# Decoder layer, expert stage: gate and up products with the expert's weights as stationary operand

## The chip, the cores and the metric

One NeuronCore of one Trainium2 chip runs the whole program in one launch. The metric is the device time of one execution in microseconds (us), the median of three runs. A product here is one matmul on TensorE: a stationary operand of 128x128 is loaded into the array (LDWEIGHTS), then the moving operand streams through, column by column, and the sum goes to a bank of PSUM.

## The reference, cut to what matters

One post-norm decoder layer on 32 sequences of 64 tokens (2048 tokens, width 512): self attention, cross attention, then a mixture of experts. Only the last part is touched.

```python
scores = jax.nn.sigmoid(x @ gate_w.T) + bias
topk_w, topk_idx = jax.lax.top_k(scores, TOPK)          # 4 of 16 experts
topk_w = topk_w / (jnp.sum(topk_w, axis=-1, keepdims=True) + 1e-20)
cw = jnp.sum(jax.nn.one_hot(topk_idx, E, dtype=x.dtype) * topk_w[..., None], axis=1)
g = jnp.einsum('th,eih->eti', x, Wg)                    # h 512, i 256
u = jnp.einsum('th,eih->eti', x, Wu)
z = jax.nn.silu(g) * u
zw = z * cw.T[:, :, None]
out = jnp.einsum('eti,ehi->th', zw, Wd)
out = out + jax.nn.silu(x @ Sg.T) * (x @ Su.T) @ Sd.T
```

## The kernel before, in words

Every product is made of three float16 ones: each operand is split into a high and a low half, and `three_pass` (lines 284 to 291) adds high by high (line 288), high by low (289) and low by high (290) into one bank, for each block of the contraction.

The expert stage works on 79 tiles of 128 picks, sorted by expert; each tile belongs to one expert. Which expert that is, is known only on the chip, since the routing has just computed it. The weights of four experts lie in a ring in SBUF (`m.ring`; per expert `2 * EW` elements, high half then low half). Table `m.place` says at which offset of the ring the tile's expert stands. TensorE's sequencer reads an entry of it into a register (`weights`, line 2041: a table load and two more operations), and every slice of the weights is addressed by that register plus a constant, which costs the sequencer an address operation in its instruction stream (ISA in the listings below, FUSED_REGOPS in the trace).

All 79 steps are written out, one after the other. Step s on TensorE, in this order:
- `gate_and_up(s)` (line 2043 on): waits for the tile's turned tokens `m.xth`, `m.xtl` (lines 2050, 2051), then 12 products with the tokens as stationary operand (128 features x 128 tokens) and 512 columns of weights moving (256 of gate, 256 of up), into one bank `GU`. After the first six the place of the next tile is loaded.
- `turn_rows` for tile s + 2 (line 1509): eight products with an identity turn the gathered rows of tokens, into `XH` and `XL`. They wait for the gather and for the copies of the last turning (lines 2088, 2089).
- `down(s - 1)` (line 2060 on): waits for zh and zl of the tile before, then six products, weights moving, 512 columns, into bank `Y`.
- `turn_z(s)` (line 2070 on): waits for z, then two float32 products with an identity turn z, tokens by features, into features by tokens, in bank `ZT`.

Beside it, in this order per step, ScalarE: silu of the gate half out of `GU` (line 1991), copy of `XH` to `m.xth` (1997), every other step Y times the pick's weight (2000), copy of `ZT` to zh (2002). VectorE: z = up times silu (2015), copy of `XL` to `m.xtl` (2019), the pick's weight (2022, 2024), every other step Y (2028), zl = `ZT` - zh (2030). GpSimd issues the gather of rows for tile s + 4 (1499) and the scatter-add of Y (1977). SyncE loads the next expert's weights (1495) when a ring slot is free, that is when TensorE has ended the last tile of the expert that had it; table `m.free` holds the event count for that.

The order between engines is kept by one counting semaphore per engine (`Timeline`): each engine marks its events in a fixed order, and others wait for a count.

Of the kernel before, what the change touches and what calls it, by code (L numbers as in the profile page):

```python
# [24 lines left out]
P = 128  # L25
# [4 lines left out]
KD = D // P  # L30
# [4 lines left out]
NE, TOPK, FI = 16, 4, 256  # L35
IB = FI // P
# [60 lines left out]
def events(per_step, extra=(), steps=NQ):  # L97

    out = []
    for q in range(steps):  # L100
        for name in per_step:
            out.append((q, name))
            for qq, after, names in extra:
                if qq == q and after == name:
                    out += [(q, x) for x in names]
    return out


def build(nc, x, xT, cT, maskf, wqT, wkT, wvT, b3, woT, bo, xwq, xwk, xwv, xwo,
# [3 lines left out]
    with top:  # L113
# [3 lines left out]
        def sem(name):  # L117
            return top.enter_context(nc.semaphore(name))
# [1397 lines left out]
        def route_and_shared(m, ln, ctx):  # L1516
# [135 lines left out]
            def vector(dve):  # L1652
# [128 lines left out]
                wait(dve, PE, "owners")  # L1781
                then(dve.tensor_copy(own[:, :], bank[1][0:1, 0:NTILES + 2]))
                dve.tensor_scalar(m.need[:, :], own[:, :], 16.0, 16.0, ALU.mult, ALU.add)
                dve.tensor_scalar(m.free[:, :], end[0:1, :], 4.0, 19.0, ALU.mult, ALU.add)
                floor_of_quotient(third[:, :], own[:, :], RING)
                then(dve.scalar_tensor_tensor(own[:, :], third[:, :], -float(RING), own[:, :], ALU.mult, ALU.add))
                dve.memset(m.place[:, 0:1], 0)
# [105 lines left out]
        def experts(m, ln):  # L1893
# [3 lines left out]
            with ExitStack() as ctx:  # L1897
# [4 lines left out]
                zh, zl = ([b(f"{n}{j}", [P, IB, P], F16) for j in range(2)] for n in ("zh", "zl"))  # L1902
                yo = [raw_front[:, j * D:(j + 1) * D] for j in range(U)]
                s_yo = [sem(f"mo_s_yo{j}") for j in range(U)]
                XH, XL, GU, ZT, Y = bank[0], bank[1], [bank[2], bank[3]], [bank[4], bank[5]], [bank[6], bank[7]]

                def per_step(names, odd):

                    return [(q, n) for q in range(U) for n in names if n != "y" or q % 2 == odd]
                PE = Timeline(sem("mo_pe"), events(["gu", "turn", "y", "zt"], steps=U), 0, [], U)  # L1910
                AC = Timeline(sem("mo_act"), per_step(["si", "xh", "y", "zh"], 1), 0, [], U)
                DV = Timeline(sem("mo_dve"), per_step(["z", "xl", "wp", "ws", "y", "zl"], 0), 0, [], U)
                assert LAST.q % 2
# [5 lines left out]
                def turns(s):  # L1919

                    return s + 2 < NTILES
# [19 lines left out]
                @block.sync  # L1941
                def _(sp):
                    routing.sync(sp)
                    routing.wait(sp, routing.DV, "tables")
                    for e in range(RING, NE):
                        sp.wait_ge(m.s_w, 16 * e)
                        done = sp.value_load(m.free[0:1, e - RING:e - RING + 1], min_val=23, max_val=4 * NTILES + 19)
                        sp.wait_ge(PE.sem, done)
                        met(sp)
                        expert_weights(sp, m, e)  # L1950
                    sp.wait_ge(m.s_w, 16 * NE)
                    combined.sync(sp, s_yo)
# [29 lines left out]
                @block.scalar  # L1982
                def _(act):
                    routing.scalar(act)
                    AC.start(act)
                    routing.wait(act, routing.DV, "tables")

                    for s in range(NTILES):
                        st, par = step(s), s % 2
                        act.wait_ge(PE.sem, PE.value("gu", st))  # L1990
                        AC.mark(act.activation(sg[par][:, :], GU[par][:, 0:FI], ACT.Silu, scale=1 / WS), "si", st, () if turns(s) else ("xh",))  # L1991
                        if turns(s):
                            loaded = act.value_load(m.need[0:1, s + 2:s + 3], min_val=16, max_val=16 * NE)
                            act.wait_ge(m.s_w, loaded)
                            met(act)
                            act.wait_ge(PE.sem, PE.value("turn", st))
                            AC.mark(act.activation(m.xth[par][:, :, :].rearrange("p k t -> p (k t)"), XH[:, :], ACT.Copy), "xh", st)
                        if out_of(st) is AC:
                            act.wait_ge(PE.sem, PE.value("y", st))
                            AC.mark(act.activation(stored(act, s - 1)[:, :], Y[(s + 1) % 2][:, :], ACT.Copy, scale=weight(act, s - 1)), "y", st)  # L2000
                        act.wait_ge(PE.sem, PE.value("zt", st))
                        AC.mark(act.activation(zh[par][:, :, :].rearrange("p n t -> p (n t)"), ZT[par][:, 0:FI], ACT.Copy), "zh", st)
                    act.wait_ge(PE.sem, PE.value("y", LAST))
                    AC.mark(act.activation(stored(act, NTILES - 1)[:, :], Y[(NTILES + 1) % 2][:, :], ACT.Copy, scale=weight(act, NTILES - 1)),
                            "si", LAST, ("xh", "y"))
                    combined.scalar(act)

                @block.vector
                def _(dve):
                    routing.vector(dve)  # L2010
                    DV.start(dve)
                    for s in range(NTILES):
                        st, par = step(s), s % 2
                        dve.wait_ge(AC.sem, AC.value("si", st))
                        i = dve.scalar_tensor_tensor(z[par][:, :], GU[par][:, FI:2 * FI], OS / WS, sg[par][:, :], ALU.mult, ALU.mult)  # L2015
                        DV.mark(i, "z", st, () if turns(s) else ("xl", "wp", "ws"))
                        if turns(s):
                            dve.wait_ge(PE.sem, PE.value("turn", st))
                            i = dve.tensor_copy(m.xtl[par][:, :, :].rearrange("p k t -> p (k t)"), XL[:, :])
                            DV.mark(i, "xl", st)  # L2020
                            t = s + 2
                            DV.mark(dve.tensor_tensor(m.of_pick[:, t % 2, :], weights_of(m, t), m.which[:, t, :], ALU.mult), "wp", st)
                            dve.wait_ge(DV.sem, DV.value("wp", st))
                            i = dve.tensor_reduce(m.weight[:, t % U:t % U + 1], m.of_pick[:, t % 2, :], AX.X, ALU.add)
                            DV.mark(i, "ws", st, ("y",) if s == 0 else ())
                        if out_of(st) is DV and s:
                            dve.wait_ge(PE.sem, PE.value("y", st))
                            DV.mark(dve.tensor_scalar(stored(dve, s - 1)[:, :], Y[(s + 1) % 2][:, :], weight(dve, s - 1), None, ALU.mult), "y", st)
                        dve.wait_ge(AC.sem, AC.value("zh", st))
                        DV.mark(dve.tensor_tensor(zl[par][:, :, :].rearrange("p n t -> p (n t)"), ZT[par][:, 0:FI],  # L2030
                                                  zh[par][:, :, :].rearrange("p n t -> p (n t)"), ALU.subtract), "zl", st)
                    combined.vector(dve)

                @block.tensor
                def _(pe):
# [7 lines left out]
                    def gate_and_up(s, w):  # L2043

                        st, par = step(s), s % 2
                        if s < 2:
                            routing.wait(pe, routing.AC, f"xh{s}")
                            routing.wait(pe, routing.DV, f"xl{s}")
                        else:
                            pe.wait_ge(AC.sem, AC.value("xh", st, 2))  # L2050
                            pe.wait_ge(DV.sem, DV.value("xl", st, 2))
                        n = 2 * FI
                        pairs = [(m.xth[par][:, k, :], m.xtl[par][:, k, :], w[:, k * n:(k + 1) * n], w[:, EW + k * n:EW + (k + 1) * n])
                                 for k in range(KD)]
                        three_pass(pe, GU[par][:, :], pairs[:2], stop=False)
                        following = weights(s + 1) if s + 1 < NTILES else None
                        mm = three_pass(pe, GU[par][:, :], pairs[2:], start=False)
                        PE.mark(mm, "gu", st, () if turns(s) else ("turn",))
                        return following

                    def down(s, w, before=()):
# [4 lines left out]
                                                            w[:, EW + c + n * D:EW + c + (n + 1) * D]) for n in range(IB)])  # L2066
                        names = (*before, "y")
                        PE.mark(mm, names[0], st, names[1:])

                    def turn_z(s):  # L2070
                        st, par = step(s), s % 2
                        pe.wait_ge(DV.sem, DV.value("z", st))
                        for n in range(IB):
                            mm = pe.transpose(ZT[par][:, n * P:(n + 1) * P], z[par][:, n * P:(n + 1) * P], ident[:, :])  # L2074
                        PE.mark(mm, "zt", st)

                    routing.wait(pe, routing.DV, "tables")
                    pe.wait_ge(m.s_w, 32)
# [1 line left out]
                    for s in range(NTILES):  # L2080
# [11 lines left out]
                        if s:  # L2092
# [2 lines left out]
                            tl = out_of(st)  # L2095
                            pe.wait_ge(tl.sem, tl.value("y", st, 2))
                            down(s - 1, before)
                        turn_z(s)
                        before, w = w, following
                    tl = out_of(LAST)  # L2100
                    pe.wait_ge(tl.sem, tl.value("y", LAST, 2))
                    down(NTILES - 1, before, ("gu", "turn"))

        def combine_and_normalise(m):

# [215 lines left out]
```

## Time and profile before

| what | value |
|---|---|
| median of three runs | 1801.9 us (1801.45 to 1802.96) |
| span of the profiled execution, first to last instruction | 1799.8 us |
| what lies around the span, by the median | 2.1 us |
| mean granted TensorE clock | 0.980 of full speed |
| TensorE busy | 1704.9 us, 95% of the span |
| expert stage, first to last product on expert weights | 1391.4 to about 1758.5 us |

The span is that of one execution; the profiled execution has no total of its own beside it, so the 2.1 us are the difference to the median of the three timed runs. A product's duration in the trace includes its way through the array: one with 512 columns shows 0.38 us, but the next starts 0.216 us after it. So the pace is read from the distance between starts. Of a sequencer's instructions, which the busy columns don't count, the duration is what it executes, and again the distance between starts is what it costs.

### The profile page before, as it was taken

Reading aid. Unit: us, or ns where it says so; the run is one execution under the profiler, and the core shown is the slowest. Engines: PE = TensorE matmul, PEld = TensorE weight load, DVE = VectorE, ACT = ScalarE, POOL = GpSimd, SP = SyncE. Lnnn points to the kernel's source line nnn. Section 1 sums busy time; section 2 is a strip of 40 time slices with the busy share of each in tenths; the row PEclk is TensorE's granted clock in tenths of the full one; section 3 lists DMA queues with packets and bytes.
Section 4 is the critical chain, followed back from the end, with each engine's and each line's share of the span. In section 5 each row is a group of like instructions: output and inputs, shape, how many; then the busy total and the mean of one; then the engine's idle time right before and its main releaser. Section 6 shows DMA issues by size and latency. Waiting matters only on the chain. (4 is left out here: it accounts for less than half of the span.)

```text
span 1799.8 us, 38774 instructions
## 1 busy us (share of the span) xinstructions
PE 1704.9 (95%) x15285; PEld 983.5 (55%) x15285; DVE 1318.8 (73%) x2251; ACT 919.3 (51%) x1545; POOL 899.9 (50%) x731
## 2 busy tenths in 40 slices
PE   6999999899999999999999999999799999899990
PEld 4676766465555555555555555555454555455550
DVE  5778789678888888888888888888879444444445
ACT  5566656665646564555455555555731333333335
POOL 7643034555645555546455555465531555555550
PEclk9999999999999999999999999999989999999995
DMA  9720020211412213214122131122144678887669
GB/s 253 173 49 20 8 62 3 92 68 53 131 61 98 85 63 98 85 58 131 64 79 87 43 104 62 56 87 70 66 165 138 152 153 217 204 225 153 118 101 298
DMA packets 84945, 190.40 MB, mean 106 GB/s; under 512 B 10848, under 2 KB 29664, under 8 KB 82720
## 3 DMA queue, kind: packets, MB, share of 16 engines
q1 hardware_dynamic: 61104, 129.44, 21.3%
q0 software_dynamic: 23088, 58.37, 16.0%
q8 instruction: 126, 2.06, 0.5%
q14 instruction: 51, 0.42, 0.1%
q10 hardware_dynamic: 576, 0.11, 0.0%
HBM read 124.68 MB, written 63.21 MB: 104 GB/s over the span
## 5 line engine op out<-in xcount | busy, mean ns | idle before, releaser
L288 PE MATMUL bank<-xhl,front_h 128*128 128x512 f16 x704 | 269.4, 383 | 11.6 <-DVE front_l L409 10.5
L289 PE MATMUL bank<-xhl,front_h 128*128 128x512 f16 x704 | 269.0, 382 | 0.0
L290 PE MATMUL bank<-xhl,front_l 128*128 128x512 f16 x704 | 268.8, 382 | 0.0
L1047 POOL TENSOR_TENSOR xa_xs<-xa_xs,sn 128x512 f32<-128x512 f32 x160 | 232.0, 1450 | 45.8 <-ACT xa_xs L1099 45.8
L1058 POOL TENSOR_TENSOR xa_sc<-xa_sc,xa_rs 128x1024 f32<-128x1024 f32 x32 | 60.8, 1901 | 374.1 <-DVE xa_rs L1312 374.1
L1052 POOL TENSOR_TENSOR xa_rr<-xa_x,xa_xs 128x512 f32<-128x512 f32 x160 | 233.1, 1457 | 12.7 <-DVE xa_x L1207 0.2
L288 PE MATMUL bank<-out_h,xa_oh 128*128 128x512 f16 x512 | 194.1, 379 | 10.7 <-DVE xa_ol L1189 7.0
L1977 POOL DMA_INDIRECT scratch_y<-raw_front,moe_to x79 | 125.3, 1586 | 144.9 <-DVE mo_zl L2030 119.7
L290 PE MATMUL bank<-out_h,xa_ol 128*128 128x512 f16 x512 | 194.0, 379 | 0.0
L289 PE MATMUL bank<-out_l,xa_oh 128*128 128x512 f16 x512 | 194.0, 379 | 0.0
L1098 ACT ACTIVATE xa_xs<-bank 64x512 f32<-64x512 f32 x160 | 94.9, 593 | 131.0 <-PE bank L290 126.7
L1207 DVE TENSOR_TENSOR xa_x<-bank,cs 128x512 f32<-128x512 f32 x160 | 109.5, 686 | 64.8 <-ACT xa_xs L1099 60.2
L1212 DVE TENSOR_TENSOR xa_rql<-xa_rr,xa_rqh 128x512 f16<-128x512 f32 x128 | 141.5, 1105 | 12.2 <-ACT xa_rqh L1105 11.6
L1155 ACT ACTIVATE xa_sc<-xa_sc 128x512 f32<-128x512 f32 x64 | 40.2, 629 | 205.9 <-DVE xa_sc L1227 205.9
L2015 DVE SCALAR_TENSOR_TENSOR raw_out<-bank,raw_out 128x256 f32<-128x256 f32 x79 | 33.6, 425 | 149.9 <-ACT raw_out L1991 143.5
L288 PE MATMUL bank<-moe_ring,moe_xth 128*128 x316 | 119.8, 379 | 0.0
L289 PE MATMUL bank<-moe_ring,moe_xth 128*128 x316 | 119.8, 379 | 0.0
L290 PE MATMUL bank<-moe_ring,moe_xtl 128*128 x316 | 119.8, 379 | 0.0
L288 PEld LDWEIGHTS bank<-xhl,front_h 128*128 128x128 f16 x704 | 69.3, 98 | 90.5 <-issue 14.0
L290 PEld LDWEIGHTS bank<-xhl,front_l 128*128 128x128 f16 x704 | 69.3, 99 | 84.7 <-issue 2.8
L1199 DVE SCALAR_TENSOR_TENSOR acc<-bank,acc 128x512 f32<-128x512 f32 x128 | 85.8, 671 | 37.1 <-PE bank L290 37.1
L289 PEld LDWEIGHTS bank<-xhl,front_h 128*128 128x128 f16 x704 | 69.4, 99 | 78.4 <-issue 2.2
(304 smaller groups left out, 4670.1 us busy)
## 6 DMA issues: line engine op xcount, KB each, us to landing
xa_rawc<-in_ew SPq DMA_DIRECT2D x32, 768.0 KB, 5.6
moe_ring<-scratch_w SPq DMA_DIRECT2D x16, 1536.0 KB
scratch_w<-xa_chunk_h SPq DMA_DIRECT2D x32, 384.0 KB, 2.3
scratch_w<-xa_chunk_l SPq DMA_DIRECT2D x32, 384.0 KB, 3.3
raw_front<-in_xwq SPq DMA_DIRECT2D x8, 1024.0 KB, 7.9
raw_out<-in_xwo SPq DMA_DIRECT2D x8, 1024.0 KB, 5.3
scratch_y<-xa_zero SPq DMA_DIRECT2D x18, 256.0 KB, 5.8
acc<-in_x POOLq DMA_DIRECT2D x4, 1024.0 KB, 10.0
```

The costliest lines, as they stand in the source:

```text
L288: pe.matmul(out_ap, ah, bh, start=start and m == 0, stop=False)
L289: pe.matmul(out_ap, ah, bl, start=False, stop=False)
L290: mm = pe.matmul(out_ap, al, bh, start=False, stop=stop and m == n - 1)
L1047: PO.mark(pool.tensor_tensor(xr, xr, sn[:, :].rearrange("p (a s) -> p a s", a=1) .to_broadcast([P, QT // S, S]), ALU.mult), f"sm{r}", st)
L1052: PO.mark(pool.tensor_tensor(rr[r % 2][:, :], x0[r % 3][:, :], xs[r % 3][:, :], ALU.add), f"ra{r}", st)
L1058: PO.mark(pool.tensor_tensor(s4, s4, rs[:, :, :].rearrange("p h (t a) -> p (h t) a", a=1) .to_broadcast([P, 16, S]), ALU.mult), "nm", st)
L1098: act.activation(xs[r % 3][0:64, :], src[64:128, :], ACT.Copy)
L1155: AC.mark(act.activation(s2, s2, ACT.Exp, scale=float(HD2) ** -0.5), f"ex{h}", st, ("ch",) if (i, q, h) == (NG - 1, NQ - 1, 1) else ())
L1199: DV.mark(dve.scalar_tensor_tensor(row, home[f"w{t}"][:, :], 1 / (WS * OS), row, ALU.mult, ALU.add), f"w{t}", st, also)
L1207: DV.mark(dve.tensor_tensor(xr, home_of(r, st)[:, :].rearrange("p (a s) -> p a s", s=S), cs[:, :].rearrange("p (a s) -> p a s", a=1) .to_b ...
L1212: DV.mark(dve.tensor_tensor(rotated(rkl, rql, r), rr[r % 2][:, :].rearrange("p (a s) -> p a s", s=S), rotated(rkh, rqh, r), ALU.subtract), ...
L1977: pool.indirect_dma_start((ya, yb)[t % 2][:, :], bass.IndirectOffsetOnAxis(m.to[:, t:t + 1], 0), y[:, :], None, compute_op=ALU.add).then_i ...
```

## The change

Gate and up swap their operands. The weights are now stationary (128 features of the input x 128 features of the output), the tile's turned tokens move (128 columns). So g and u come out as features by tokens, which is how the down products want z, and nothing turns z any more: `turn_z` and the bank pair `ZT` go. Gate gets a bank of its own and an event of its own ("g"), up another. ScalarE makes zh from z itself, VectorE subtracts it from z. The order of events on TensorE is now g, gu, turn, y, so the count in `m.free` moves by one.

```diff
-                XH, XL, GU, ZT, Y = bank[0], bank[1], [bank[2], bank[3]], [bank[4], bank[5]], [bank[6], bank[7]]
+                XH, XL, G, UP, Y = bank[0], bank[1], [bank[2], bank[3]], [bank[4], bank[5]], [bank[6], bank[7]]
...
-                PE = Timeline(sem("mo_pe"), events(["gu", "turn", "y", "zt"], steps=U), 0, [], U)
+                PE = Timeline(sem("mo_pe"), events(["g", "gu", "turn", "y"], steps=U), 0, [], U)
...
-                        act.wait_ge(PE.sem, PE.value("gu", st))
-                        AC.mark(act.activation(sg[par][:, :], GU[par][:, 0:FI], ACT.Silu, scale=1 / WS), "si", st, () if turns(s) else ("xh",))
+                        act.wait_ge(PE.sem, PE.value("g", st))
+                        AC.mark(act.activation(sg[par][:, :], G[par][:, 0:FI], ACT.Silu, scale=1 / WS), "si", st, () if turns(s) else ("xh",))
...
-                        act.wait_ge(PE.sem, PE.value("zt", st))
-                        AC.mark(act.activation(zh[par][:, :, :].rearrange("p n t -> p (n t)"), ZT[par][:, 0:FI], ACT.Copy), "zh", st)
+                        act.wait_ge(DV.sem, DV.value("z", st))
+                        AC.mark(act.activation(zh[par][:, :, :].rearrange("p n t -> p (n t)"), z[par][:, :], ACT.Copy), "zh", st)
...
+                        dve.wait_ge(PE.sem, PE.value("gu", st))
                         dve.wait_ge(AC.sem, AC.value("si", st))
-                        i = dve.scalar_tensor_tensor(z[par][:, :], GU[par][:, FI:2 * FI], OS / WS, sg[par][:, :], ALU.mult, ALU.mult)
+                        i = dve.scalar_tensor_tensor(z[par][:, :], UP[par][:, 0:FI], OS / WS, sg[par][:, :], ALU.mult, ALU.mult)
...
-                        n = 2 * FI
-                        pairs = [(m.xth[par][:, k, :], m.xtl[par][:, k, :], w[:, k * n:(k + 1) * n], w[:, EW + k * n:EW + (k + 1) * n])
-                                 for k in range(KD)]
-                        three_pass(pe, GU[par][:, :], pairs[:2], stop=False)
+
+                        def features(o, c):
+                            return three_pass(pe, o, [(w[:, c + k * 2 * FI:c + k * 2 * FI + P], w[:, EW + c + k * 2 * FI:EW + c + k * 2 * FI + P],
+                                                       m.xth[par][:, k, :], m.xtl[par][:, k, :]) for k in range(KD)])
+                        for n in range(IB):
+                            mm = features(G[par][:, n * P:(n + 1) * P], n * P)
+                        PE.mark(mm, "g", st)
                         following = weights(s + 1) if s + 1 < NTILES else None
-                        mm = three_pass(pe, GU[par][:, :], pairs[2:], start=False)
+                        for n in range(IB):
+                            mm = features(UP[par][:, n * P:(n + 1) * P], FI + n * P)
                         PE.mark(mm, "gu", st, () if turns(s) else ("turn",))
...
-                    def turn_z(s):
-                        st, par = step(s), s % 2
-                        pe.wait_ge(DV.sem, DV.value("z", st))
-                        for n in range(IB):
-                            mm = pe.transpose(ZT[par][:, n * P:(n + 1) * P], z[par][:, n * P:(n + 1) * P], ident[:, :])
-                        PE.mark(mm, "zt", st)
```

The instructions of TensorE in gate and up, before: the second half of step 2, behind the load of the next tile's place (moe_ring is the weight ring, moe_xth and moe_xtl the turned tokens, in SBUF; ISA is a sequencer instruction).

```order
L2041 TENSOR_LOAD moe_place
L2041 ISA x2
L288 ISA
L288 MATMUL bank<-moe_ring,moe_xth 128x512
L289 ISA
L289 MATMUL bank<-moe_ring,moe_xth 128x512
L290 MATMUL bank<-moe_ring,moe_xtl 128x512
L288 ISA
L288 MATMUL bank<-moe_ring,moe_xth 128x512
L289 ISA
L289 MATMUL bank<-moe_ring,moe_xth 128x512
L290 MATMUL bank<-moe_ring,moe_xtl 128x512
```

The same place now, its first two groups of eight:

```order
L2042 TENSOR_LOAD moe_place
L2042 ISA x2
L288 ISA
L288 MATMUL bank<-moe_xth,moe_ring 128x128
L289 MATMUL bank<-moe_xtl,moe_ring 128x128
L290 ISA
L290 MATMUL bank<-moe_xth,moe_ring 128x128
L288 ISA
L288 MATMUL bank<-moe_xth,moe_ring 128x128
L289 MATMUL bank<-moe_xtl,moe_ring 128x128
L290 ISA
L290 MATMUL bank<-moe_xth,moe_ring 128x128
```

A group of three products has two address operations in both; behind the table load there were two such groups, and there are eight, and ahead of it as many again. Over the whole program TensorE's listing has 1106 ISA operations before and 3002 now, 14 and 38 per tile.

From the last down products of a step to the next gate, before:

```order
L288 ISA
L288 MATMUL bank<-moe_ring,mo_zh 128x512
L289 ISA
L289 MATMUL bank<-moe_ring,mo_zh 128x512
L290 MATMUL bank<-moe_ring,mo_zl 128x512
L2074 MATMUL bank<-ident,raw_out 128x128 [waits mo_dve]
L2074 MATMUL bank<-ident,raw_out 128x128
L288 ISA [waits mo_dve,mo_act]
L288 MATMUL bank<-moe_ring,moe_xth 128x512
```

and now:

```order
L288 ISA
L288 MATMUL bank<-moe_ring,mo_zh 128x512
L289 ISA
L289 MATMUL bank<-moe_ring,mo_zh 128x512
L290 MATMUL bank<-moe_ring,mo_zl 128x512
L288 ISA [waits mo_dve,mo_act]
L288 MATMUL bank<-moe_xth,moe_ring 128x128
```

The two turnings of z (raw_out is z's buffer) with their wait for VectorE are gone; the next gate follows the down products at once.

## Rows read from the trace of the kernel before

Line numbers are those of the kernel before. PE is TensorE, PEld its weight loads, PEldq its sequencer, DVE VectorE. Times of one instruction are in ns, starts in us from the start of the span.

**Rows 1.** The page, part 1: busy us, share of the span, instructions by engine
```profile
PE 1704.9 (95%) x15285; PEld 983.5 (55%) x15285; DVE 1318.8 (73%) x2251; ACT 919.3 (51%) x1545; POOL 899.9 (50%) x731
```

**Rows 2.** Expert stage: length, busy us by engine (x count), PEclk, DMA share, GB/s
```profile
1391.40:1758.50 367.10, 360.43 (x2197) 192.75 (x2195) 158.90 (x437) 128.47 (x274) 197.54 (x153) 1.00 0.74 167
```

**Rows 3.** Instructions on the expert weights, ns min/median/max, first and last start
```profile
L288 PEld LDWEIGHTS bank<-moe_ring,moe_xth x316: 95/98/98, 1391.2 to 1753.3; 128*128 128x128 f16 x158
L288 PE MATMUL bank<-moe_ring,moe_xth x316: 379/379/387, 1391.4 to 1753.5; 128*128 x158
...
L290 PE MATMUL bank<-moe_ring,mo_zl x158: 379/379/379, 1398.9 to 1758.1; 128*128 x158
```

**Rows 4.** TensorE in order of time, one step: start us, us, line, tiles
```profile
1500.12 0.38 PE L288 MATMUL bank<-moe_ring,moe_xth 128*128 x1
...
1502.71 0.61 PE L1509 MATMUL bank<-identh,moe_rows 128*128 128x128 f16 x8
1503.16 0.38 PE L288 MATMUL bank<-moe_ring,mo_zh 128*128 x1
...
1504.45 0.38 PE L2074 MATMUL bank<-ident,raw_out 128*128 128x128 f32 x2
1504.67 0.38 PE L288 MATMUL bank<-moe_ring,moe_xth 128*128 x1
```

**Rows 5.** TensorE in order of time, cross attention: a run of 48 narrow products
```profile
906.46 0.23 PE L288 MATMUL bank<-front_h,ch 128*128 128x128 f16 x1
...
909.15 0.38 PE L288 MATMUL bank<-out_h,xa_oh 128*128 128x512 f16 x1
```

**Rows 6.** TensorE's sequencer by line: table load overall, then one stretch of a step
```profile
L2041 PEldq TENSOR_LOAD <-moe_place x79: 298/487/967, 1389.3 to 1747.2; - x79
L2051 PEldq EVENT_SEMAPHORE  x1: 51/51/51, 1503.8 to 1503.8; - x1
L288 PEldq FUSED_REGOPS  x2: 42/44/46, 1503.9 to 1504.2; - x2
L289 PEldq FUSED_REGOPS  x2: 46/46/46, 1504.0 to 1504.3; - x2
L2041 PEldq TENSOR_LOAD <-moe_place x1: 498/498/498, 1504.4 to 1504.4; - x1
L288 PEldq FUSED_REGOPS  x2: 46/46/46, 1505.2 to 1505.6; - x2
L289 PEldq FUSED_REGOPS  x2: 46/46/46, 1505.4 to 1505.7; - x2
L2089 PEldq EVENT_SEMAPHORE  x1: 51/51/51, 1505.8 to 1505.8; - x1
```

**Rows 7.** The same, from the turning of rows to the next step; last row VectorE
```profile
L2089 PEldq EVENT_SEMAPHORE  x1: 51/51/51, 1465.0 to 1465.0; - x1
L2064 PEldq EVENT_SEMAPHORE  x1: 51/51/51, 1465.2 to 1465.2; - x1
L288 PEldq FUSED_REGOPS  x2: 46/46/46, 1465.3 to 1465.5; - x2
L2051 PEldq EVENT_SEMAPHORE  x1: 51/51/51, 1467.4 to 1467.4; - x1
L2015 DVE SCALAR_TENSOR_TENSOR raw_out<-bank,raw_out x1: 424/424/424, 1466.9 to 1466.9; 128x256 f32<-128x256 f32 x1
```

**Rows 8.** What TensorE waited for in the expert stage: us, times, longest
```profile
PE bank L1509 <- issue: 3.5, 2, 1.9
PE bank L288 <- DVE mo_zl L2030: 2.3, 3, 1.1
```

**Rows 9.** Stretches of 2, 5 and 10 us: same columns as rows 2
```profile
308.00:310.00 2.00, 0.35 (x15) 0.38 (x16) 2.00 (x4) 1.99 (x3) 0.00 (x0) 1.00 0.00 0
310.00:315.00 5.00, 5.00 (x107) 4.96 (x105) 4.32 (x10) 1.06 (x2) 0.00 (x0) 0.51 0.01 3
1290.00:1300.00 10.00, 6.82 (x48) 3.35 (x48) 9.96 (x19) 5.16 (x8) 4.93 (x6) 1.00 0.30 105
```

More of the change, by code:

```diff
@@ L1783, in vector @@
                 dve.tensor_scalar(m.need[:, :], own[:, :], 16.0, 16.0, ALU.mult, ALU.add)
-                dve.tensor_scalar(m.free[:, :], end[0:1, :], 4.0, 19.0, ALU.mult, ALU.add)
+                dve.tensor_scalar(m.free[:, :], end[0:1, :], 4.0, 20.0, ALU.mult, ALU.add)
                 floor_of_quotient(third[:, :], own[:, :], RING)
@@ L1946, in _ @@
                         sp.wait_ge(m.s_w, 16 * e)
-                        done = sp.value_load(m.free[0:1, e - RING:e - RING + 1], min_val=23, max_val=4 * NTILES + 19)
+                        done = sp.value_load(m.free[0:1, e - RING:e - RING + 1], min_val=24, max_val=4 * NTILES + 20)
                         sp.wait_ge(PE.sem, done)
@@ L2029, in _ @@
                         dve.wait_ge(AC.sem, AC.value("zh", st))
-                        DV.mark(dve.tensor_tensor(zl[par][:, :, :].rearrange("p n t -> p (n t)"), ZT[par][:, 0:FI],
+                        DV.mark(dve.tensor_tensor(zl[par][:, :, :].rearrange("p n t -> p (n t)"), z[par][:, :],
                                                   zh[par][:, :, :].rearrange("p n t -> p (n t)"), ALU.subtract), "zl", st)
@@ L2097, in _ @@
                             down(s - 1, before)
-                        turn_z(s)
                         before, w = w, following
@@ L2101, in _ @@
                     pe.wait_ge(tl.sem, tl.value("y", LAST, 2))
-                    down(NTILES - 1, before, ("gu", "turn"))
+                    down(NTILES - 1, before, ("g", "gu", "turn"))
         def combine_and_normalise(m):
```

## The prediction

> **What bounds the kernel now.** I read the page first. TensorE is busy 95% of the span [rows 1], so time is won or lost on TensorE's way through the program. Then the table of stretches: the change touches the expert stage alone, and that stage runs from 1391.4 us to 1758.5 us, 367.1 us, with TensorE busy for 360.4 of them, VectorE 158.9, ScalarE 128.5, GpSimd 197.5, the clock at 1.00 [rows 2]. The first gate-and-up product and the last down product are its ends [rows 3]. Over 79 steps VectorE works 2.0 us a step, ScalarE 1.6, GpSimd 2.5.
>
> Third, TensorE in order of time, for one step. Twelve wide products take from 1500.12 to 1502.71, 2.59 us, 0.216 us each; the eight turnings of rows 0.45 us; six down products 1.29 us; the two turnings of z 0.22 us; the next step begins at 1504.67 [rows 4]. A step is 4.55 us and has no hole. 79 of them make 359.5 us, so 7.6 us of the stage are stalls, such as the 3.5 us before line 1509 [rows 8].
>
> Fourth, and this decides: the same engine's sequencer, the unit that reads the instruction stream and hands products and weight loads to the array. Its own instructions appear as PEldq. The busy columns leave them out. For each expert weight that is addressed through a register it runs one address operation (FUSED_REGOPS) of 46 ns. In the half with nothing to wait for, these start at 1503.9, 1504.0, 1504.2, 1504.3, and the table load follows at 1504.4 [rows 6]: 0.125 us apart, whether one product stands between two of them or two. After the load come four more, from 1505.2 to the event at 1505.8. The eight take 1.1 us together, **0.13 us each**; the load with what belongs to it takes 0.8 us (1504.4 to 1505.2). Together with the event ahead of them that is 2.0 us for gate and up. From the turning of rows to the down products' wait it is 0.2 us more, for that wait and four address operations 0.6 (0.1 to the first of them, then 4 x 0.13) [rows 7]. So the sequencer works 2.8 us in a step of 4.55. The rest it stands: at 1467.4 it goes on just after VectorE has ended z (1466.9 + 0.42) [rows 7]. Today it has 1.75 us to spare, and is nowhere seen.
>
> **The change, part by part.** (1) Gate and up: 12 products with 512 moving columns become 48 with 128. Cross attention has exactly such a run, 48 products of 128x128, each with its own load: 906.46 to 909.15, 2.69 us, 0.056 each [rows 5]. So the array needs 0.10 us more than the 2.59.
> (2) The turnings of z go: -0.22 us on the array, and TensorE's wait for z with them. The array's step is 4.55 + 0.10 - 0.22 = 4.43 us.
> (3) Address operations. Each group of three products has two (one for the weights' high half, one for the low). There were 4 groups in gate and up, there are 16: 8 operations become 32, as the two order excerpts show. 24 more at 0.13 us is 3.1 us of sequencer per step: **2.8 + 3.1 = 5.9 us**. This is longer than the array's 4.43, so the sequencer sets the step. Its order hides nothing: the array's down products and turnings, 1.74 us, run while it prepares the next gate products, and in gate and up a group of three costs it 0.26 us against 0.17 for the array, so the array catches up and stands.
> (4) What the trace cannot show is a weight load addressed through a register. Today the product's moving side is so addressed and the load's side is not. Lower bound: no more than now, since one product or two in a slot cost the same [rows 6]. Below that, the 12 register-addressed products that go could give back what is bounded next: from the event to the first address operation it is 0.1 us [rows 6, 7], against 0.125 with products between, so the products and loads of a slot cost 0.025 us; 12 times that is 0.3 us a step, 24 us in all. Upper bound: each of the 48 loads costs as much, 1.2 us a step, 95 us in all. I take nothing, as both kinds of slot read alike, and keep a third of the upper end for the range.
> (5) Sigmoid-weighted gate, z, zh and zl: ScalarE may start with the gate half before up is done, and z is read from SBUF instead of PSUM. Nothing is on the path: zl of a step is wanted only by the down products after the next step's gate and up, VectorE and ScalarE have 2.0 and 1.6 us of work in at least 4.43, and TensorE waited for zl 2.3 us in the whole stage [rows 8]. Priced at nothing; if VectorE took 0.4 us longer for it, it still had 2 us.
> (6) Four banks and the event numbers (20 for 19): an expert's weights are released after the same down products. The weight loads issued by SyncE, the gathers and scatters of GpSimd are the same in number and come later with a slower step; GpSimd's 2.5 us of 5.9 hides them. The 7.6 us of stalls vanish: their DMAs get 1.35 us more per step.
>
> **Sum.** 79 x 5.9 = 466.1 us in the place of 367.1: +99 us. Against the profiled execution's span, 1799.8 becomes 1898.8; with the 2.1 us that the median of the three runs, 1801.9, lies above it, **1901 us**.
>
> A page bears on (1). The trace has 0.056 us for a narrow product with its load. The Trainium skill, TensorE: Matmul & The Clock Gate, section "Back-to-back issue gap", says that a sustained stream of load and product takes some 81 ns each at 128 columns; the trace does not agree. By the page the array's step would be 4.33 + 48 x 0.081 - 2.59 = 5.6 us, still under the sequencer's 5.9, so the forecast would stay; only rival A would come to about 1880.
>
> **Rivals.** A, faster: the address operations hide. If the sequencer's 0.13 us is not a cost of each operation but slack that it takes only when the array is fed anyway, the array sets the step at 4.43: 79 x -0.12 = -9 us, **1793 us**. It decides below (4.43 - 2.8) / 24 = 0.07 us per operation. For it: 46 ns is all that the operation itself lasts. Against it: behind the event at 1503.8, with no wait in between, eight in a row keep that spacing, and the two after the event at 1465.2 do too [rows 6, 7]; nothing held them back but themselves. Chance 0.06. The Trainium skill, Advanced Engine Details and Errata, "Sequencer Loop", would side with it: other engine instructions can be read and queued while a control instruction executes. That one product or two fit a slot of the same length agrees with it; that the slot is 0.125 us does not.
> B, slower still: loads no longer hide. A weight load lasts 98 ns [rows 3]; if a register-addressed one cannot be pulled ahead, 48 x 0.098 = 4.7 us in the place of 2.59, step 6.44, 79 x 6.44 = 509 us: **1944 us**. Against it the static run of rows 5. Chance 0.04.
> C: the clock. With the array busy 4.43 of 5.9 us, 75%, the granted clock might fall to its lower level of 1.2 GHz. The narrow run would take twice its time, and the whole array step 8.9 us: 703 us, **2138 us**. In the trace the clock fell to half after 2 us with the array busy 0.35 (308 to 310, then 0.51), while 10 us with 6.8 busy stayed at 1.00 [rows 9]. Chance 0.03.
>
> **Chances and range.** The forecast has 0.86. A measurement of this kernel tells 0.2% from no change; all cases but A lie far above. Within 0.2% I give 0.01. Faster 0.06, same 0.01, slower 0.93. The forecast's own range: 24 operations at 0.125 and always the shortest table load, 0.3 for 0.5 [rows 6], give 2.6 + 3.0 = 5.6 us a step, 1877, and the lower bound of (4) less than that; a third of its upper bound gives 1933. The range is 1868 to 1938; outside lie A, B, C and what remains of the forecast's edges, 2 in 10.
>
> **What would show it.** Right: the step in TensorE's order of time is 5.8 to 6.0 us; the FUSED_REGOPS of lines 288 and 290 stand 0.125 us apart through all of gate and up with no pause; narrow products come in twos and ones with holes between; TensorE's busy time in the stage falls well under the stage's length; the waits for weight DMAs are gone; the clock stays 1.00. Wrong: narrow products 0.056 us apart and a 4.4 us step (A), products 0.1 us apart at evenly spaced loads (B), or PEclk at 5 in the stage (C). If the pause at the z event is still there, something that I count as hidden is not.

## The result, and the profile after

The changed kernel takes **1891.2 us** (median of 4 runs, 1889.54 to 1892.07) beside 1802.4 us for the kernel before on the same chip: ratio 1.0491, 95% interval 1.0475 to 1.0506. It is slower by 88.7 us, by 4.9%. The forecast was 1901, the range 1868 to 1938.

The page of the kernel after, part 1, which answers to [rows 1]; a row of part 5; and its stretch from the first gate product to the last down product, which answers to [rows 2]:

```profile
PE 1765.7 (94%) x17971; PEld 1110.2 (59%) x17971; DVE 1326.4 (70%) x2251; ACT 918.6 (49%) x1545; POOL 899.7 (48%) x731
...
L288 PE MATMUL bank<-moe_xth,moe_ring 128*128 128x128 f16 x1264 | 254.0, 223 | 33.6 <-issue 33.0
```

```profile
1389.50:1848.20 458.70, 422.49 (x4883) 320.83 (x4881) 165.77 (x437) 127.01 (x274) 197.49 (x153) 1.00 0.61 134
```

The stage has grown from 367.1 to 458.7 us, 91.6; the span by 87.9 (1887.7 for 1799.8). So the whole loss is in this stage, and the rest of the program is some 4 us shorter. ScalarE and GpSimd have the work that they had, VectorE 7 us more; the clock stands at 1.00. TensorE shows 422 us of work, 92%, and 33 us of idle time put down to "issue". Read by itself that would be an engine that is nearly full. It is not, as its order of time shows. Up's products of one step, and the next turning of rows:

```profile
1505.61 0.22 PE L289 MATMUL bank<-moe_xtl,moe_ring 128*128 128x128 f16 x1
1505.66 0.22 PE L290 MATMUL bank<-moe_xth,moe_ring 128*128 128x128 f16 x1
1506.34 0.23 PE L288 MATMUL bank<-moe_xth,moe_ring 128*128 128x128 f16 x1 [0.46 <-issue]
1506.40 0.22 PE L289 MATMUL bank<-moe_xtl,moe_ring 128*128 128x128 f16 x1
1506.46 0.23 PE L290 MATMUL bank<-moe_xth,moe_ring 128*128 128x128 f16 x1
1506.59 0.23 PE L288 MATMUL bank<-moe_xth,moe_ring 128*128 128x128 f16 x1
...
1506.87 0.23 PE L288 MATMUL bank<-moe_xth,moe_ring 128*128 128x128 f16 x1
...
1508.41 0.61 PE L1509 MATMUL bank<-identh,moe_rows 128*128 128x128 f16 x8
```

Up to 1505.66 the products stand 0.056 us apart: the array works off what the sequencer prepared during the down products. The next one comes 0.68 us later. From there on a group of three comes every 0.25 to 0.28 us (1506.34, 1506.59, 1506.87) where it needs 0.17. Each product still shows 0.22 us, its way through the array, so the holes between starts count as busy. The only hole the wait list shows is the one at 1506.34, once per step:

```profile
PE bank L288 <- issue: 33.0, 78, 0.8
PE bank L288 <- DVE mo_zl L2031: 2.2, 3, 1.4
```

The waits that stood there before [rows 8] are the wait for zl, as long as it was, and the one before line 1509, which is gone. The sequencer, by line, in the same step (the table load is line 2042 now, the turning's wait 2087, the down products' wait 2069, the next gate's wait 2052); it answers to [rows 6, 7]:

```profile
L2042 PEldq TENSOR_LOAD <-moe_place x79: 296/301/568, 1387.6 to 1836.0; - x79
...
L2042 PEldq TENSOR_LOAD <-moe_place x1: 300/300/300, 1505.6 to 1505.6; - x1
L2042 PEldq FUSED_REGOPS  x1: 151/151/151, 1506.0 to 1506.0; - x1
L2042 PEldq SEQ_ASSERT  x1: 18/18/18, 1506.2 to 1506.2; - x1
...
L288 PEldq FUSED_REGOPS  x8: 46/46/46, 1506.2 to 1508.1; - x8
...
L290 PEldq FUSED_REGOPS  x8: 46/46/46, 1506.4 to 1508.2; - x8
...
L2087 PEldq EVENT_SEMAPHORE  x1: 51/51/51, 1508.3 to 1508.3; - x1
...
L2069 PEldq EVENT_SEMAPHORE  x1: 51/51/51, 1508.4 to 1508.4; - x1
...
L2052 PEldq EVENT_SEMAPHORE  x2: 51/51/51, 1503.3 to 1509.1; - x2
```

From one event of line 2052 to the next, 1503.3 to 1509.1, the sequencer goes from one instruction to the next with no wait in its rows. Sixteen address operations fill 1506.2 to 1508.3, 0.13 us each, though one lasts 46 ns. Most follow each other at 0.124 us; between 1400 and 1730 us, 1650 of the 1878 distances are 0.12 us, the others 0.13 to 0.31, and the mean is 0.132. What lengthens the others was not tried. The turning of rows starts at 1502.64 in one step and at 1508.41 in the next: a step of 5.77 us for 4.55 [rows 4]. The median over the stage is 5.76.

### The profile page after: what moved, and what is told of

The parts are those of the page before. It is cut to its first block and busy times, and to the rows that moved or that the text cites. A ratio compares the mean times of both kernels' runs of the same rounds, so it can differ in the third digit from the quotient of the medians.

```text
span 1887.7 us, 46119 instructions
## 1 busy us (share of the span) xinstructions
PE 1765.7 (94%) x17971; PEld 1110.2 (59%) x17971; DVE 1326.4 (70%) x2251; ACT 918.6 (49%) x1545; POOL 899.7 (48%) x731
## 5 line engine op out<-in xcount | busy, mean ns | idle before, releaser
L288 PE MATMUL bank<-moe_xth,moe_ring 128*128 128x128 f16 x1264 | 254.0, 223 | 33.6 <-issue 33.0
L290 PE MATMUL bank<-moe_xth,moe_ring 128*128 128x128 f16 x1264 | 254.0, 223 | 0.0
L289 PE MATMUL bank<-moe_xtl,moe_ring 128*128 128x128 f16 x1264 | 248.7, 219 | 0.0
L288 PEld LDWEIGHTS bank<-moe_xth,moe_ring 128*128 x1264 | 122.2, 97 | 76.2 <-issue 47.9
L1997 ACT ACTIVATE moe_xth<-bank 128x512 f16<-128x512 f32 x77 | 46.0, 597 | 216.3 <-PE bank L1509 200.8
L289 PEld LDWEIGHTS bank<-moe_xtl,moe_ring 128*128 x1264 | 124.1, 98 | 9.2
L290 PEld LDWEIGHTS bank<-moe_xth,moe_ring 128*128 x1264 | 122.2, 97 | 10.1 <-issue 1.2
```

What stands on the lines that cost most here:

```text
L288: pe.matmul(out_ap, ah, bh, start=start and m == 0, stop=False)
L289: pe.matmul(out_ap, ah, bl, start=False, stop=False)
L290: mm = pe.matmul(out_ap, al, bh, start=False, stop=stop and m == n - 1)
```

## The experiments

The theory: **the sequencer's in-order work is the step.** Rivals: the register-addressed weight load itself is slow; the 3792 narrow products with their loads that stand in the place of 948 wide ones are slow; the turning of z that went, or its wait, did something. Each kernel was run beside the kernel before on the same chip; "step" is the median distance over the stage from one turning of rows (line 1509) to the next. The kernels that take fixed weights or drop the turning of z leave a part of the computation out, so they show where the time goes and are no candidates.

### No registers at all, in either kernel

`after_fixed` takes the weights of the stage from buffers at fixed addresses (those of an earlier part), in gate, up and down, and reads no table; `before_fixed` does the same to the kernel before.

```diff
-    return three_pass(pe, o, [(w[:, c + k * 2 * FI:c + k * 2 * FI + P], w[:, EW + c + k * 2 * FI:EW + c + k * 2 * FI + P],
+    return three_pass(pe, o, [(front_h[:, c + k * 2 * FI:c + k * 2 * FI + P], front_l[:, c + k * 2 * FI:c + k * 2 * FI + P],
...
-    return m.ring[:, bass.ds(pe.value_load(m.place[0:1, s + 1:s + 2], min_val=0, max_val=(RING - 1) * 2 * EW), 2 * EW)]
+    return None
...
```

> The changed kernel, but gate, up and down take their weights from fixed places in SBUF (the shared expert's, the same for every tile) instead of the ring slot that the register names; the table load of each step is gone too. The routed experts' own weights are so left out of the computation. The same products, loads, waits and banks otherwise. Theory S (the sequencer's address operations set the step): nothing is left for the sequencer, the array sets the step at 4.43 us, 9 us under the kernel before: 1793 us. Rival L (48 narrow products cost more on the array than the static run in cross attention, because their loads do not hide here): the time stays near 1891. Rival B (something in banks, ScalarE or VectorE holds the step at 5.76): near 1891 too.

> The kernel before with the same edit: fixed weights, no address operations, no table load; the routed experts' own weights are left out. Its sequencer had 1.75 us to spare in a step, so theory S says no change: 1802 us, within 3. If register-addressed products were slow in themselves, or table load and address operations cost something in the kernel before too, it is faster.

Measured: `after_fixed` 1795.0 beside 1800.9, ratio 0.9966 (0.9952 to 0.998), step 4.42; `before_fixed` 1801.3 beside 1800.9, ratio 1.0 (0.999 to 1.0009), step 4.55. The turnings of rows in order of time, `after_fixed`:

```profile
1641.21 0.61 PE L1509 MATMUL bank<-identh,moe_rows 128*128 128x128 f16 x8
...
1645.63 0.61 PE L1509 MATMUL bank<-identh,moe_rows 128*128 128x128 f16 x8
```

The loss is in the addressing, all of it: without it the array's step is the 4.42 us that parts (1) and (2) of the prediction work out to 4.43. And the kernel before loses nothing to its sequencer. The pace gained, 0.13 x 79 = 10 us, comes out as 6: the turning of rows now waits for gathers (1.6 us, 0.2 before) and once for "issue" (4.2, 3.5 before), which is about half of the 4 us that are missing; the rest is not traced.

### Registers in the instructions, or the operations that fill them

`after_no_load` loads one register before the stage and computes the addresses in the code once; the loads and products of gate, up and down are still addressed by register. `after_one_slice` reads the table at each step as the changed kernel does, but takes one and the same slice of the expert's weights in all 16 groups.

```diff
# after_no_load
+    if s == 0:
+        at = pe.value_load(m.place[0:1, 0:1], min_val=0, max_val=512)
+        fixed.append((front_h[:, bass.ds(at, KD * 2 * FI)], front_l[:, bass.ds(at, KD * 2 * FI)],
+                      out_h[:, bass.ds(at, IB * D)], out_l[:, bass.ds(at, IB * D)]))
+    return None
# after_one_slice
-    return three_pass(pe, o, [(w[:, c + k * 2 * FI:c + k * 2 * FI + P], w[:, EW + c + k * 2 * FI:EW + c + k * 2 * FI + P],
+    return three_pass(pe, o, [(w[:, 0:P], w[:, 0:P],
```

> The changed kernel with every weight slice still addressed through a register, but through one register that is loaded once (with 0), so that the addresses are computed once, in the first step, and reused in all others: 79 steps with register-addressed loads and products and with neither table loads nor address operations. The routed experts' own weights are left out. Theory S: as the fixed one, 1793 us. Rival R (it is the register-addressed weight load that is slow, not the operation that computes its address): near 1891.

> The changed kernel with the table load of every step and the register of the ring slot, but all 48 products of gate and up take one slice of the weights (the first), so that no address operation is needed for them; those of down stay. What is left out: the other slices of gate and up. Theory S: sequencer 5.76 - 32 x 0.125 = 1.8 us a step, the array sets 4.43: 1793 us, or up to 8 more where the table load (0.66 us in which nothing is handed on) comes when the array has little in its queue. If the table load, not the address operations, made the step, it stays above 1850.

Measured: 1795.0, ratio 0.9963 (0.9948 to 0.9977), and 1793.7, ratio 0.9952 (0.9935 to 0.997); step 4.42 in both, as with fixed addresses. `after_no_load` in order of time and on its sequencer:

```profile
1640.70 0.61 PE L1509 MATMUL bank<-identh,moe_rows 128*128 128x128 f16 x8
...
1645.12 0.61 PE L1509 MATMUL bank<-identh,moe_rows 128*128 128x128 f16 x8
```

```profile
L2044 PEldq TENSOR_LOAD <-moe_place x1: 487/487/487, 1386.1 to 1386.1; - x1
```

A weight load addressed by a register costs the array nothing: 48 of them a step run at the static pace. That closes the unknown of part (4) at the value taken, zero, as far as the array goes, and rules rival B out; of the sequencer it shows that these loads never made it the limit here. `after_one_slice` has the table load and the narrow products but one address operation a step in gate and up: it is these.

### How much each address operation costs

In these five kernels some of the 16 groups of a step take fixed addresses, and the rest stay. A group is two operations; c is its column block (0 and 128 gate, 256 and 384 up), k its block of the contraction.

```diff
-    return three_pass(pe, o, [(w[:, c + k * 2 * FI:c + k * 2 * FI + P], w[:, EW + c + k * 2 * FI:EW + c + k * 2 * FI + P],
-                               m.xth[par][:, k, :], m.xtl[par][:, k, :]) for k in range(KD)])
+    return three_pass(pe, o, [((front_h[:, c + k * 2 * FI:c + k * 2 * FI + P], front_l[:, c + k * 2 * FI:c + k * 2 * FI + P])
+                               if c == 0 and k < 2 else (w[:, c + k * 2 * FI:c + k * 2 * FI + P], w[:, EW + c + k * 2 * FI:EW + c + k * 2 * FI + P]))
+                              + (m.xth[par][:, k, :], m.xtl[par][:, k, :]) for k in range(KD)])
```

The condition is `c == 0 and k < 2` in `after_4_fewer`, `c == 0` in `after_8_fewer`, `c < FI` in `after_16_fewer`: groups in one run from gate's start.

> The changed kernel with 4 of its 32 gate and up address operations taken away per step: the first two blocks of the first gate half take fixed weights (the shared expert's; the routed ones are left out there). Theory S, each operation 0.125 to 0.13 us in a step that the sequencer sets: 79 x 4 x 0.13 = 41 us less, 1850 us. Rivals in which the sequencer does not set the step: 1891.

> The same with 8 operations fewer (all of the first gate half fixed). Theory S: a step of 5.76 - 1.03 = 4.73 us, still above the array's 4.43: 82 us less, 1809 us, a few more if weight DMAs come late again as in the kernel before. A straight line with the run of 4 fewer shows that each operation costs the same.

> The same with 16 operations fewer (all of gate fixed, up through the register). Theory S: the sequencer would need 3.7 us, the array needs 4.43, so the line ends: 1793 to 1800 us, not the 1727 of the straight line. If it goes on below 1780, the array's part was sized wrong.

Measured:

| kernel | operations fewer | us | ratio (95%) | step |
|---|---|---|---|---|
| changed kernel | 0 | 1891.2 | 1.0491 (1.0475 to 1.0506) | 5.76 |
| `after_4_fewer` | 4 | 1853.8 | 1.0291 (1.0263 to 1.0318) | 5.29 |
| `after_8_fewer` | 8 | 1846.0 | 1.0243 (1.0217 to 1.0269) | 5.20 |
| `after_16_fewer` | 16 | 1832.3 | 1.0168 (1.0141 to 1.0195) | 4.95 |

Four fewer save (1891.2 - 1853.8) / (4 x 79) = 0.118 us each. Eight and sixteen fewer **miss** by 37 and by over 30 us: the next four save only 0.02 each. The theory as put, a sum of sequencer work without regard to its place, falls. The sequencer of `after_8_fewer` tells why. The first of its address operations in one step; twelve fixed products of gate stand before them:

```profile
L288 PEldq FUSED_REGOPS  x2: 46/46/46, 1501.8 to 1502.1; - x2
...
L290 PEldq FUSED_REGOPS  x1: 46/46/46, 1502.0 to 1502.0; - x1
...
L290 PEldq FUSED_REGOPS  x1: 46/46/46, 1502.6 to 1502.6; - x1
...
L288 PEldq FUSED_REGOPS  x1: 46/46/46, 1502.8 to 1502.8; - x1
```

and its array at that time:

```profile
1502.54 0.38 PE L290 MATMUL bank<-moe_ring,mo_zl 128*128 x1
1502.76 0.22 PE L288 MATMUL bank<-moe_xth,front_h 128*128 128x128 f16 x1
```

After 1502.1 the sequencer stands until 1502.6 with nothing to wait for but the array. It has then handed on 12 + 3 + 2 = 17 products of gate, and the array has just started the last down product; when the array starts the next product, at 1502.76, the sequencer takes its next one. In `after_16_fewer` it has handed on all 24 fixed products of gate before it gets to the table load:

```profile
L2042 PEldq TENSOR_LOAD <-moe_place x1: 297/297/297, 1510.5 to 1510.5; - x1
...
L2042 PEldq SEQ_ASSERT  x1: 18/18/18, 1511.1 to 1511.1; - x1
```

```profile
1510.47 0.22 PE L290 MATMUL bank<-moe_xth,front_l 128*128 128x128 f16 x1
1510.53 0.22 PE L288 MATMUL bank<-moe_xth,front_h 128*128 128x128 f16 x1
...
1511.98 0.22 PE L290 MATMUL bank<-moe_xth,moe_ring 128*128 128x128 f16 x1
1512.08 0.23 PE L288 MATMUL bank<-moe_xth,moe_ring 128*128 128x128 f16 x1
...
1512.32 0.23 PE L288 MATMUL bank<-moe_xth,moe_ring 128*128 128x128 f16 x1
```

The load starts at 1510.5, as the array starts the seventh gate product: again 24 - 7 = 17 ahead. From the event at 1509.1 to the load 1.4 us go by. Handing on the 24 products takes some 0.2 us of them (an estimate: in `after_8_fewer` the event of line 2052 and twelve products take 0.20 us, 1501.64 to 1501.84, and the event alone 0.11 in the changed kernel); the other 1.2 us the sequencer stands, and in up the array stands again (0.24 us from group to group at 1512.08). So the sequencer can be about 17 products ahead of the array and no more. `after_fixed`, whose sequencer nothing else holds up, has the same number in every step: in all 72 steps between 1400 and 1730 us the event ahead of the turning of rows comes when exactly 17 products before that turning have not started. One of them, and the first and last of the 17:

```profile
L2087 PEldq EVENT_SEMAPHORE  x2: 51/51/51, 1640.2 to 1644.6; - x2
```

```profile
1644.68 0.22 PE L289 MATMUL bank<-moe_xtl,front_h 128*128 128x128 f16 x1
...
1645.57 0.22 PE L290 MATMUL bank<-moe_xth,front_l 128*128 128x128 f16 x1
```

Seventeen narrow products are 17 x 0.056 = 0.95 us of cover; time saved in one run of fixed groups is lost above that.

If this holds, the same number of operations taken out at even distances must save in full. `after_8_spread` has the condition `k == 0`, `after_16_spread` `k % 2 == 0`.

> Again 8 address operations fewer than the changed kernel, but spread: in each of the four halves of gate and up the first of four blocks takes fixed weights (the routed ones are left out there), instead of the whole first gate half. Theory Q (the sequencer can lead the array by some 16 to 18 products only, so a run of narrow products without operations makes it wait, and that time is lost to the operations behind it): three narrow products without operations at a time hold nobody up, the straight line of 0.13 us each returns, a step of 5.76 - 1.03 = 4.73 us, 1809 to 1815 us, against 1846 for the 8 in one run. Rival (an operation costs less when there are fewer of them, or something else ends the step near 5.0): 1846 again.

> Again 16 address operations fewer, but spread: every other block takes fixed weights. Theory Q: two blocks cost the sequencer 0.26 us and the array 0.34, so the sequencer keeps its lead, of which the table load takes 0.66 us; the step falls to the array's 4.43 or little above, 1795 to 1803 us, against 1832 for the 16 in one run. Rival as above: 1832 again.

Measured: 1819.8, ratio 1.0093 (1.0077 to 1.011), step 4.82, and 1796.7, ratio 0.9963 (0.9948 to 0.9978), step 4.42. Eight operations in one run gave back 45 us, eight spread 71; sixteen 59 and 95. In order of time, `after_8_spread`:

```profile
1640.97 0.61 PE L1509 MATMUL bank<-identh,moe_rows 128*128 128x128 f16 x8
...
1645.78 0.61 PE L1509 MATMUL bank<-identh,moe_rows 128*128 128x128 f16 x8
```

(5.76 - 4.82) / 8 = 0.118 us an operation again, which is why eight spread ended some 5 us above the band given (worked out with 0.13). Sixteen spread reach the floor of the array: 5.76 - 16 x 0.118 = 3.9 us of sequencer are under 4.42.

### A second table load

`after_two_loads` reads the table once more in each step, in the same place.

```diff
     following = weights(s + 1) if s + 1 < NTILES else None
+    w = weights(s)
```

> The changed kernel with a second table load per step: the place of the tile is loaded anew ahead of up, with the same value and the same result. Theory S: it adds what the first costs the sequencer, 0.66 us (1505.59 to 1506.24 in the changed kernel's trace), to each of 79 steps: 52 us, 1943 us. If the load hides behind queued products, nothing: 1891.

Measured: 1941.9, ratio 1.0776 (1.0748 to 1.0804), step 6.39 in the median. The load with its two operations costs (6.39 - 5.76) = 0.63 us, 50 us over 79 steps, in full: the second suspected cost of the sequencer behaves as the first.

### The turning of z

`after_turn` puts the two turnings of z and TensorE's wait for z back into the changed kernel (into an unused half of gate's bank; nobody reads them). `before_no_turn` takes them out of the kernel before; ScalarE and VectorE make zh and zl from z itself, as in the change, though here z lies tokens by features, so the transposition is left out.

```diff
# after_turn
         down(s - 1, before)
+    turn_z(s)
...
+        pe.transpose(G[par][:, FI + n * P:FI + (n + 1) * P], z[par][:, n * P:(n + 1) * P], ident[:, :])
# before_no_turn
-    pe.wait_ge(DV.sem, DV.value("z", st))
-    for n in range(IB):
-        mm = pe.transpose(ZT[par][:, n * P:(n + 1) * P], z[par][:, n * P:(n + 1) * P], ident[:, :])
-    PE.mark(mm, "zt", st)
```

> The changed kernel with the two float32 turnings of z and their wait for VectorE put back at their old place, into an unused part of the gate bank; nobody reads them. They cost the array 0.22 us a step. Theory S: the array stands for more than a microsecond of the 5.76 us step, so they cost it nothing; the sequencer hands them on in about 0.02 us and reaches the wait for z after z is done: 1891 us, at most 3 more. If the array set the step: 79 x 0.22 = 17 us more, 1908.

> The kernel before without the turning of z: zh and zl are made from z as it lies in SBUF, which leaves the transposition out of the computation. In this kernel the array sets the step, so 0.22 us of it go in each of 79 steps: 17 us less, 1785 us, or some us more where weight DMAs come late. This is the second term of the change by itself.

Measured: `after_turn` 1892.3 beside 1800.5, ratio 1.0508 (1.0493 to 1.0522), step 5.77: 0.22 us of array work and a wait, put back, cost 0.01 us a step, as the sequencer was the bound. The two kernels' ratios, 1.0508 and 1.0491, lie 3 us apart with intervals that overlap, where the full price would be 17. `before_no_turn` 1790.4, ratio 0.9938 (0.9924 to 0.9951), step 4.33 for 4.55: there the same 0.22 us are paid in full, 17 us by the pace, but the kernel ends only 10 earlier. Of the 7 us between, 4 are waits of the stage, which have grown to those below; the other 3 are not traced:

```profile
PE bank L1509 <- issue: 5.1, 2, 3.7
PE bank L1509 <- DMA moe_rows<-scratch_x,moe_list: 3.0, 4, 1.6
PE bank L288 <- DVE mo_zl L2030: 2.1, 3, 1.4
```

## Why the prediction was right, point by point

The mechanism was the one forecast: the sequencer's in-order work takes the place of the array's as the length of a step. +88.7 us was measured, +99 forecast. Its steps:

(1), (2) Array 4.43 us a step: 4.42 measured with addresses that cost nothing (`after_fixed`). (3) 24 more address operations at 0.13 us: in the changed kernel they stand 0.132 us apart in the mean, 24 x 0.132 = 3.2 for 3.1. Taken out, one saves 0.118 (`after_4_fewer`, `after_8_spread`), which fits with the three products of its group still to be handed on, at some 0.01 us each. (4) Register-addressed loads at nothing: nothing on the array (`after_no_load`), and on the sequencer nothing beyond the slots above. (5) Silu, z, zh and zl hidden: no wait for them but the 2.2 us for zl, which were there before. (6) Banks and events: nothing. Of the 7.6 us of stalls that were to vanish, the 3.5 before the turning are gone; those for zl, 2.3 before and 2.2 now, are not.

The term that was mis-sized is the sum of the sequencer, 5.9 us where 5.76 came. The share of the table load was read from one step of the kernel before, 0.8 us with a load of 498 ns (median 487 [rows 6]). After, the load lasts 300 ns, and `after_two_loads` prices the whole at 0.63; in the step shown it is 0.65 (1505.59 to 1506.24). These 0.15 us are the whole miss: 5.76 less 0.65 for the load and 0.34 for the three events with the way to the next operation leaves 4.77 us for 36 address operations, 0.132 each, so the 0.13 was right. The step of 5.76 is just under the 5.8 to 6.0 that the prediction gave as a sign. 79 x 5.76 = 455 us, and 2.2 us of wait for zl, the stage's first products and its last bring it to 458.7; the prediction had 466.1. Of the 11.1 us by which the span came out under the forecast's 1898.8 these are 7.4; the other 3.7 are the rest of the program, and what shortened it was not tried.

Rival A fell: each operation costs the sequencer its slot, far above the 0.07 us at which A would begin. Rival B fell with `after_no_load`. Rival C did not come: the clock was 1.00 in the stage with the array busy 4.42 of 5.76 us by starts. On part (1), the static run's 0.056 us for a narrow product with its own load is also what 48 of them take here, register-addressed too; so the 81 ns of the Trainium skill, TensorE: Matmul & The Clock Gate, "Back-to-back issue gap", don't hold in this kernel.

What was wrong was said of the sequencer in the experiments: that only the sum of its work counts. In the changed kernel the limit of 17 products is not reached: in the step from 1503.3 on the sequencer is at most ten ahead. Where fixed groups were put in one run it cost 26 us for eight operations (1846.0 against 1819.8 spread) and 36 for sixteen (1832.3 against 1796.7).

No version here beats the kernel before and computes the same. The floor of the new design is 4.42 us a step against 4.55, 6 us of 1801 (`after_fixed`, `after_16_spread`), and it needs some twelve of the 38 operations of a step to go, evenly spread: (5.76 - 4.42) / 0.118 = 11.4, an estimate, as sixteen were run. Taking the turning of z out of the kernel before is worth 10 us, but needs a product whose result comes out turned, which is what the swap pays for with addresses.

## What to carry to other kernels

Count what the sequencer must do per product, not only what the array does: cutting wide products into narrow ones multiplies the address operations where operands lie at a place known only at run time, and each costs 0.12 us, the time of two narrow products. Addresses that are computed once and kept in registers cost nothing at each use: `after_no_load` runs 36 address operations in its first step and none in the 78 behind it. Whether the places of the ring could be kept so, with all 16 groups on their own weights, was not tried. Read the bound from the distance between starts and from the sequencer's own rows; the busy share showed 92% for an array that was waiting 23% of the time (4.42 us of work in 5.76). Where static and register-addressed work are mixed, spread the costly ones evenly: the sequencer's lead is short.

## What the runs showed of the hardware that was not expected

- The sequencer stands when it is about 17 products (each with its weight load) ahead of the array: in `after_8_fewer` with a wide down product running, in `after_16_fewer` with narrow ones. In `after_fixed` the event of the next gate finds 17 not yet started in 63 of 73 steps, and six of these are wide ones, so products of either width count alike there. The Trainium skill, Advanced Engine Details and Errata, "Engine Queue Depths", has 64 for TensorE; 17 pairs are 34 instructions, so the runs show about half, if a load and a product take a place each.
- An address operation lasts 46 ns and takes a slot of 0.12 us; a product or two handed on within it make it no longer. Handing on products with no operation among them is cheap, about 0.01 us each (twelve in 0.09 us, the estimate from `after_8_fewer`).
- The same table load lasts 487 ns in the median of the kernel before [rows 6], about 300 in the changed kernel and in `before_no_turn`:

```profile
L2041 PEldq TENSOR_LOAD <-moe_place x79: 296/301/897, 1389.8 to 1736.5; - x79
```

What makes it longer in the kernel before is open. Taking the turning of z out, with zh and zl made from z, brings it down; putting it back into the changed kernel (`after_turn`) leaves it at 302 ns. So neither the turning nor its wait does it alone.
